# A fused attention and expert kernel on one core: 16-bit parts in the linear and quantised stages, and unread products in two attention turns

## What is computed

```python
# quantised net, F = 512
h = (x - mu) * rsqrt(var + EPS) * ln_gamma + ln_beta
w1 = (fc1_q - 128.0) * fc1_scales           # 128 x 512
y = silu(h @ w1 + fc1_bias)
w2 = (fc2_q - 128.0) * fc2_scales           # 512 x 128
x = x + 0.5 * 0.5 * (y @ w2 + fc2_bias + ...)

# linear attention, H = 16 heads of E = 8
q, k, v = x @ q_w.T, x @ k_w.T, x @ v_w.T
lc = sigmoid(tanh(x @ cs_w1.T + cs_b1) @ cs_w2.T + cs_b2)
lam = clip(sigmoid(decay_params) * (1.0 + 0.2 * lc), 0.0, 0.9995)
state = state * lam[..., None] + k[..., None] * v[:, :, None, :]   # for each token
out = einsum('bhe,bhef->bhf', q, state)
```

## Time and profile before

| | us |
|---|---|
| median of 3 runs | 1323.84 (1322.83 to 1324.23) |
| the profiled execution, its own time | 1324.04 |
| its span, first to last instruction | 1322.3 |
| PE busy | 1092.7 (83%), 11805 products |
| DVE busy | 985.9 (75%) |
| POOL busy | 856.6 (65%) |
| ACT busy | 724.3 (55%) |

### The profile page before, as it was taken

The page is one execution under the profiler, slowest core; times in us unless marked ns, Lnnn a source line. Parts: engine busy times, 40 slices in busy tenths (PEclk is TensorE's granted clock), DMA queues, the critical chain, the costliest instruction groups (busy, mean ns, idle before and its releaser), DMA issues. The chain is left out here.

```text
span 1322.3 us, 32967 instructions
## 1 busy us (share of the span) xinstructions
PE 1092.7 (83%) x11805; PEld 819.8 (62%) x11805; DVE 985.9 (75%) x2554; ACT 724.3 (55%) x1311; POOL 856.6 (65%) x1033
## 2 busy tenths in 40 slices
PE   2753996389999999999999988579994988999697
PEld 1432775156666666666666665368883875777577
DVE  6872885588888888989898875378885936888672
ACT  4721554446667676667666676335662744444174
POOL 4874777225667688878787887544774315889651
PEclk9886998589999999999999999679997898999989
DMA  8113431011110011111011010143323100000001
GB/s 258 45 48 106 112 106 53 26 39 26 26 25 20 20 30 34 33 30 33 25 34 34 24 28 12 43 132 93 105 74 115 36 1 0 1 1 1 0 25 40
DMA packets 63980, 62.78 MB, mean 47 GB/s; under 512 B 11088, under 2 KB 53488, under 8 KB 63440
## 3 DMA queue, kind: packets, MB, share of 16 engines
q1 hardware_dynamic: 54384, 39.66, 11.4%
q0 software_dynamic: 9440, 21.02, 4.7%
HBM read 28.10 MB, written 24.17 MB: 40 GB/s over the span
## 5 line engine op out<-in xcount | busy, mean ns | idle before, releaser
L1784 ACT ACTIVATE diff_prob<-diff_st_ps 128x512 f32<-128x512 f32 x384 | 227.8, 601 | 160.9 <-PE diff_st_ps L2227 154.2
L1933 DVE TENSOR_REDUCE diff_q_pack<-diff_s_ps 128x2 f16<-128x512 f32 (+1 forms) x384 | 262.1, 692 | 63.5 <-PE diff_s_ps L2210 60.9
L1719 POOL TENSOR_SCALAR_AFFINE_SELECT diff_prob<-diff_prob 128x256 f32<-128x256 f32 (+1 forms) x384 | 188.0, 497 | 121.9 <-ACT diff_prob L1784 119.6
L431 POOL DMA_INDIRECT exp_ys<-moe_y_sb,moe_dest x156 | 152.7, 979 | 86.8 <-ACT moe_y_sb L514 54.1
L2210 PE MATMUL diff_s_ps<-diff_k_one,diff_qT 128*128 128x128 f16 (+1 forms) x1024 | 149.8, 249 | 0.0
L2227 PE MATMUL diff_st_ps<-diff_qmT,diff_k_one 128*128 128x256 f16 (+1 forms) x1024 | 147.7, 248 | 0.3 <-ACT diff_prob L1784 0.2
L2250 PE MATMUL diff_ot_ps<-diff_prob,diff_v 128*32 128x128 f32 x3072 | 125.5, 282 | 9.1 <-POOL diff_prob L1719 6.8
L507 ACT ACTIVATE moe_h_hi<-moe_h 128x512 f16<-128x512 f32 x94 | 59.2, 630 | 88.2 <-DVE moe_h L737 88.2
L1686 POOL TENSOR_TENSOR diff_rms<-diff_ms,all_neghalf 128x8 f32<-128x8 f32 x64 | 105.0, 1641 | 3.7 <-DVE diff_ms L1957 2.8
L2210 PEld LDWEIGHTS diff_s_ps<-diff_k_one,diff_qT 128*128 128x128 f16 x1024 | 90.7, 99 | 22.2 <-issue 0.7
L2250 PEld LDWEIGHTS diff_ot_ps<-diff_prob,diff_v 128*32 128x32 f32 x3072 | 73.3, 110 | 44.5 <-issue 23.3
(11 more groups left out here) (390 smaller groups left out, 3069.8 us busy)
## 6 DMA issues: line engine op xcount, KB each, us to landing
moe_xg<-exp_xs SPq DMA_DIRECT2D x78, 130.0 KB, 2.3
diff_k_one<-diff_kT SPq DMA_DIRECT2D x128, 64.0 KB, 2.0
diff_yg<-exp_ys SPq DMA_DIRECT2D x14, 256.0 KB, 3.0
fetched_yg<-exp_ys SPq DMA_DIRECT2D x7, 512.0 KB, 3.9
exp_ys<-moe_y_sb,moe_dest POOLq DMA_INDIRECT x156
all_x<-in_x SPq DMA_DIRECT2D x4, 512.0 KB, 5.1
moe_up<-in_w SPq DMA_DIRECT2D x16, 128.0 KB, 3.9
out<-all_x SPq DMA_DIRECT2D x8, 256.0 KB, 2.3
```

The lines of the kernel that those rows point to most:

```text
L431: nc.gpsimd.indirect_dma_start(out=ew.ys, out_offset=bass.IndirectOffsetOnAxis(ap=dest[:, s, j:j + 1], axis=0), in_=y_sb[:, s % YR, j], in ...
L1719: nc.gpsimd.affine_select(out=pr, in_=pr, compare_op=ALU.is_ge, fill=0.0, base=0, pattern=[[0, n], [1, P]], channel_multiplier=-1).then_in ...
L1784: nc.scalar.activation(prob[:, u % RING], st_ps[:, u % 2], ACT.Exp, scale=SCALE).then_inc(exp_ready, 1)
L1933: nc.vector.tensor_reduce(q_pack[:, par, j, m0:m0 + n, 3 * HD], s_ps[:, u % 2].rearrange("p (m k) -> p m k", m=n), op=ALU.max, axis=AX.X, ...
```

## The change

Three things are done.

1. In the quantised net and the linear attention the high and low parts are F16 instead of F32R, weights and activations alike. The number and order of products stay.
2. A helper `keep_busy(n)` issues n products 128x512 of F16 that write to `st_ps`, which nothing reads before it is written again. In the attention's turn 0 they stand at the steps of `FILL`: 5, 5, 8, 8, 9 and 4, together 39.
3. In turn 1 one such product follows the scores of each of the 24 steps.

```diff
-        self.hi1 = nm.sb("fc1_hi", [P, F], F32R)
-        self.lo1 = nm.sb("fc1_lo", [P, F], F32R)
+        self.hi1 = nm.sb("fc1_hi", [P, F], F16)
+        self.lo1 = nm.sb("fc1_lo", [P, F], F16)
...
-        hT_hi = nm.sb("hT_hi", [P, 2, GN], F32R)
-        hT_lo = nm.sb("hT_lo", [P, 2, GN], F32R)
+        hT_hi = nm.sb("hT_hi", [P, 2, GN], F16)
+        hT_lo = nm.sb("hT_lo", [P, 2, GN], F16)
...
-                nc.vector.tensor_tensor(hT_lo[:, g % 2], t_ps[:], hT_hi[:, g % 2].bitcast(F32), ALU.subtract).then_inc(hT_ready, 1)
+                nc.vector.tensor_tensor(hT_lo[:, g % 2], t_ps[:], hT_hi[:, g % 2], ALU.subtract).then_inc(hT_ready, 1)
...
+    FILL = {1: 5, 3: 5, 8: 8, 12: 8, 14: 9, 17: 4}
...
+            def keep_busy(n):
+
+                for i in range(n if ew else 0):
+                    nc.tensor.matmul(st_ps[:, i % 2], ew.ident_h[:], ew.up_hi[:, 0].rearrange("p a h -> p (a h)"), start=True, stop=True)
+
             def turn(A, B, C, D, par):
                 norms, routes, places, sends = groups(D)
                 for u in range(STEPS):
+                    if A is not None and B is None and u in FILL:
+                        keep_busy(FILL[u])
                     if B is not None:
                         scores(B, u, 1 - par)
+                        if C is None and D is None:
+                            keep_busy(1)
...
-        w_hi = nm.sb("w_hi", [P, 2 + NF, P], F32R)
-        w_lo = nm.sb("w_lo", [P, 2 + NF, P], F32R)
-        c_hi = nm.sb("c_hi", [P, CS], F32R)
-        c_lo = nm.sb("c_lo", [P, CS], F32R)
+        w_hi = nm.sb("w_hi", [P, 2 + NF, P], F16)
+        w_lo = nm.sb("w_lo", [P, 2 + NF, P], F16)
+        c_hi = nm.sb("c_hi", [P, CS], F16)
+        c_lo = nm.sb("c_lo", [P, CS], F16)
...
-        xT_hi = nm.sb("xT_hi", [P, 2, GN], F32R)
-        xT_lo = nm.sb("xT_lo", [P, 2, GN], F32R)
+        xT_hi = nm.sb("xT_hi", [P, 2, GN], F16)
+        xT_lo = nm.sb("xT_lo", [P, 2, GN], F16)
```

More of the change, by code:

```diff
@@ L711, in dequantize @@
                 dve.wait_ge(deq_own, 2)
-                nc.vector.tensor_tensor(deq.lo1[:], w1g[:], deq.hi1[:].bitcast(F32), ALU.subtract)
+                nc.vector.tensor_tensor(deq.lo1[:], w1g[:], deq.hi1[:], ALU.subtract)
             def keep_gT(s):
@@ L2650, in low @@
                 dve.wait_ge(xT_hi_ready, g + 1)
-                nc.vector.tensor_tensor(xT_lo[:, b], tkq_ps[:], xT_hi[:, b].bitcast(F32), ALU.subtract).then_inc(xT_ready, 1)
+                nc.vector.tensor_tensor(xT_lo[:, b], tkq_ps[:], xT_hi[:, b], ALU.subtract).then_inc(xT_ready, 1)
             def bound_lam(g, b):
@@ L2663, in _ @@
             once(nc.vector.tensor_copy(w_hi[:], w_in[:]))
-            once(nc.vector.tensor_tensor(w_lo[:], w_in[:], w_hi[:].bitcast(F32), ALU.subtract))
+            once(nc.vector.tensor_tensor(w_lo[:], w_in[:], w_hi[:], ALU.subtract))
             once(nc.vector.tensor_copy(c_hi[:], c_in[:]))
-            once(nc.vector.tensor_tensor(c_lo[:], c_in[:], c_hi[:].bitcast(F32), ALU.subtract))
+            once(nc.vector.tensor_tensor(c_lo[:], c_in[:], c_hi[:], ALU.subtract))
             dve.wait_ge(base_ready, 1)
```

## The result

The changed kernel takes 1318.51 us (median of 7 runs, 1315.57 to 1320.12), the kernel before 1324.23 (7 runs, 1322.83 to 1324.86) beside it: a ratio of 0.9959, 95% interval 0.995 to 0.9969. It is faster by 5.7 us, about half of the forecast 11, and 1318.51 lies just outside the range that ended at 1318.5. The run with the trace is the fastest of the seven: 1315.57, span 1313.9 against 1322.3. Read alone it shows 8.4 us, of which a part is luck; the later traces tell which.

A forecast was written before the change was run, and what follows sets the result against it. PE bounds the nets, a POOL-PE-DVE loop the linear stage, PE's bursts turn 0, mostly DVE's maxima turn 1. Savings 1.45 + 0.5 + 2.3 + 4.4 + 2.3 = 10.95 us: 1324.04 to 1313.1, median 1312.9; range 1309 to 1318.5.

The forecast's parts named there:

- (a): F16 parts on PE: a run of six products falls from 1.47 us to 1.30 to 1.33, taken as 0.17 saved.
- (b): Quantised nets: 13 full-clock runs at 0.17 us plus 0.1 at the cold start, 2.3 saved per net, 4.6 in both.
- (c): Linear attention: 0.60 us saved a round in seven rounds, plus 0.2 for the cold start, 4.4 in all.
- (d): Attention turn 0: unread products raise the clock, second projection 1.05 us and transposes of k 0.4 faster, 1.45 saved.
- (e): Attention turn 1: with 24 unread products the clock's relapses should go, 0.5 us saved, between -2 and 2.
- rival 5: Attention gains nothing or loses up to 2 us, clock falling at turn 0's end; F16 gains hold: 1315 to 1317; 15%.
- Rival 2: F16 parts: the products' pace stays, only each run's first product gains, 0.08 us a run: 1317.6; 10%.
- rival 1: Turns 0 and 1: unread products stay at 1.2 GHz and block PE, costing 13.7 us: 1328.7; 3%.
- rival 3: F16 parts change nothing, 32-bit work around them sets the pace; only the attention's 1.95 us is left: 1322.1; 5%.
- rival 4: Turn 1: the clock never falls back, DVE's waits for PE go too, up to 3 us more: 1310; 12%.

The follow-up runs named there:

- wide_c: Changed kernel with the linear stage's `hidden` weights zero-padded from 32 to 128 columns: 1316.76 us, ratio 0.995 to the kernel before.
- down_mid: Changed kernel with down(g - 1) moved right behind the four transposes of group g + 1: 1321.98 us, ratio 0.9988 to the kernel before.
- hold_no_t1: Changed kernel with padded `hidden` weights, eight more unread products at turn 0's end, none in turn 1: 1314.41 us, ratio 0.993 to the kernel before.
- f16_wide: Changed kernel without any unread products, with `hidden` weights padded to 128 columns: 1317.91 us, ratio 0.9954 to the kernel before.
- no_fill_t1: Changed kernel without turn 1's 24 unread products: 1421.19 us, ratio 0.9965, on a chip where the kernel before takes 1426 us.

## Why the prediction was half right

*The price of an F16 product (a).* 0.216 for every product of the run and 1.29 for six came true. The step that failed is the 0.17 saved per run. I took the F32R run as 1.47, from the first product's start, and counted 0.08 of its 0.31 as a price. The earlier trace rows are recorded so, but the 0.08 had already been taken from the transposes or the `down` ahead. I looked for it behind the first 16-bit product, and not at the gap ahead of it. A sum over a whole round of each kernel would have shown it. Measured: 0.10 a run, which is six times the difference of pace, 0.232 - 0.2155.

*Nets (b).* Forecast 2.3 each. Three traces with F32R in the original order have 71.90 and 69.97 on average, the eight with F16 70.53 and 68.75: 1.4 and 1.2. The rounds say the same without the spread of the starts: six distances between `down`s at 0.22 and 0.20 less. The count of 13 runs was about right, 13 x 0.10 = 1.3. PE as the bound, and no one else in the way, was right.

*Linear attention (c).* Forecast 0.60 a round, measured 17.97 - 17.73 = 0.24. Its own terms make 0.20 + 3 x (0.11 to 0.13) = 0.53 to 0.59, a little under the 0.60 taken. The 0.60 held the same false 0.08 in all four runs. By the difference of pace 18 products save 18 x 0.0166 = 0.30 (an estimate), and the two open weight loads, which are in no row of before, cost 0.18 of it: 0.12 is left. The other 0.12 is not PE's. POOL waits twice in a round, 1.28 + 0.35 us before and 1.10 + 0.41 after; what is left of the round, POOL's own work, fell from 16.34 to 16.22. Its 128x512 multiplications take 1.28 to 1.29 us on average in the four F32R traces and 1.27 in the ten F16 ones, twelve a round. Why they are shorter no run shows. So the loop was half right: PE is on it, since wide_c takes 0.22 off the stretch and 0.20 off the round, but by way of ACT's copy of v as well as by the scan, and POOL's own time moved though the prediction held it fixed. With the loads covered the saving is 17.97 - 17.53 = 0.44. The whole stage gave 162.13 - 159.96 = 2.2 (means of three and six traces) against 4.4: 1.7 in the rounds and 0.5 in the start, which hangs on when the clock rises (the first state and q product comes 14.2 to 15.4 us after the stage's start with F16, 15.1 to 15.5 with F32R).

*Turn 0 (d).* In the first trace the clock was full at the second projection as forecast, the projection gained 1.07 (forecast 1.05), the transposes of k came 1.07 earlier, and the first piece of the k transfer 1.48 earlier, where both terms forecast 1.45. What failed is the last link, "on the path through ACT's copy and the k transfer": one of SP's four issues took 1.28 us instead of 0.59, and 0.79 was left. An issue of 1.0 to 1.7 us instead of 0.6 stands in all five traces in which the first piece was issued 16.7 us into the turn, and in one of the nine with a later one (down_mid); why is open. Nor did the clock hold in every trace: of the nine with turn 0's products, DVE has the second projection's result after 9.7 us in five, after 10.32 and 10.60 in two, and in down_mid and hold_no_t1 after 10.75 as in the kernel before, because the clock had fallen back to 0.50 ahead of it. Six traces with the fill of both turns average 21.71 (21.23 to 22.81) against 22.24 in five without: 0.5.

*Turn 1 (e).* 29.25 against 29.93 on average: 0.7 saved (forecast 0.5). That the number fits is luck as much as insight: the traces with the products run from 28.3 to 30.8, within my bounds of -2 to 2, those without from 29.3 to 30.4, and 0.7 is not clear of that spread.

*What I left out.* "From turn 2 on nothing is changed" is true of the instructions and was false of the time. Turns 2 to 14 average 452.36 in the six traces with the fill of both turns, 451.27 in the five with none: 1.1 us given back, 0.6 of it in turn 5 (34.75 against 34.14, where f16_wide's collision counts among those with none) and 0.2 in turn 7. Attention as a whole gains 0.5 + 0.7 - 1.1 = 0.1, where 1.95 was forecast. For the attention that is the outcome of rival 5, to which I gave 15%. Its mechanism, a clock that falls at the end of turn 0 and scores that start cold, is seen, but it cost little on average; what took the gain back are the turns from 2 on, which no rival named.

So two terms of the sum were mis-sized at their root, the price of a product in (b) and (c), and one effect was put at nothing without a reason, that of the shifted turns from 2 on. The terms as measured, 0.1 + 1.4 + 2.2 + 1.2, make 4.9, under the 5.7 of the medians by less than the spread of either. Rival 2 (1317.6) comes near the measured time by accident: it kept the first product's gain and denied the pace, where the runs show the pace and no gain of the first. The rule of the Trainium skill that I weighed there, page "TensorE: Matmul & The Clock Gate", section "Weight-path perf modes — Fast Weight Load (FWL) and DoubleRow", that the array takes one element per cell and cycle whatever its width, would have F16 and F32R run alike. The traces do not agree: 0.2155 against 0.232 a product. Rivals 1, 3 and 4 did not occur; rival 1's mechanism, unread products that run cold and hold PE up, is seen in turn 1 of wide_c and down_mid, at some 1 to 2 us and not 13.7.

## What to carry to other kernels

Price a change of PE's work from one whole round, start to same start, and never from the first record of a run alone: a record may be displaced against its neighbours, and then what is gained behind it is lost ahead of it. Where a saving shifts one engine against another, compare the untouched turns behind it as well, since a collision that is there or not by 0.2 us costs as much as the saving brought. Products that only keep the clock up help the work that follows them at once: a pause behind them can give the clock back, so look for the last pause ahead of the work that must be fast, and then measure, since a fast start of turn 1 did not make turns 0 and 1 shorter here. And follow a saving to the last issue of a transfer, not to the first.

## What the runs showed of the hardware

- F32R products 128x512 run at 0.232 us and F16 ones at 0.2155. Going back and forth between F16 products and 32-bit ones costs nothing: one, two or three entries a group leave 6.60 us.
- A change between F16 weights of 128 and of 32 columns leaves the weight load open, 0.09 us each time. F32R weights show none of it. Padding to 128 columns gained 0.20 us a round.
- A DVE multiplication of two SBUF operands takes 0.52 us, or 1.36 behind a POOL multiplication that began 0.18 us before it. It ends 0.28 us after POOL's, in turn 5 as in turns 3, 4, 6 and 7.
- In six traces with a pause of PE of 1.3 to 2.3 us ahead of turn 1, the granted clock fell to 0.50 in the pause or within 0.9 us behind it, and was back 2.7 to 5.7 us after the first score, with the same order of the attention's products in all six. In the two traces with products in the pause it stayed at 1.00. What decides how long it stays down is open.
- One of SP's four issues of the k transfer took 1.28 us instead of 0.59 in the changed kernel, and up to 1.70 in no_fill_t1; the first score starts 2.15 us after the fourth. Why the issue is held up is open.
- POOL's multiplications in the linear stage take 1.27 us in all ten traces with F16 parts and 1.28 to 1.29 in the four with F32R. Why is open.
